# MLP residual seeded into PSUM, biases as bf16 products, layer norms on ScalarE, key products first, one table for Exp and Ln

## The reference

```python
# embedding: four tiers of rows, each with its own scale row, quantised to 16, 8, 6, 4 bits
scale = max(max(abs(tw[i] * ts[i])), 1e-8) / max_val        # over the whole tier
table = where(tier 0, tw * ts, clip(round(tw * ts / scale)) * scale)
x = layernorm(take(table, ids))
# mixer of a state space kind
proj = rms(x) @ in_proj_w.T                 # zgate 512, u 512, B 16, C 16, dt 8
xBC = silu(conv4(u, B, C))                  # 4 taps along the sequence
B, C = B * rsqrt(sum(B*B)), C * rsqrt(sum(C*C)); d = softplus(dt + dt_bias)
z = (z + d * (u*B - A*y)) / (1 + d*d*A); y = y + d * z;  out_t = y @ C     # 128 steps
x = x + ((out + D_skip*u) * silu(zgate)) @ out_proj_w.T + out_proj_b
# MLP, layer norm, quantised linear layer
x = x + gelu(rms(x) @ fc1_w.T + fc1_b) @ fc2_w.T + fc2_b
h = h + quantised_linear(layernorm(h))      # activation scale from the maximum over all rows
```

## Time and profile before

| | us |
|---|---|
| three runs | 1417.49, 1417.96, 1420.06 |
| median | 1417.96 |
| the profiled execution's own time | 1418.98 |
| its span, first to last instruction | 1417.2 |
| granted TensorE clock, mean | 0.954 |
| busy: TensorE, VectorE, ScalarE, GpSimd | 1148.7, 1181.0, 755.9, 802.1 |

### The profile page before, as it was taken

The page is one execution under the profiler, slowest core; times in us unless marked ns, Lnnn a source line. Parts: engine busy times, 40 slices in busy tenths (PEclk is TensorE's granted clock), DMA queues, the critical chain, the costliest instruction groups (busy, mean ns, idle before and its releaser), DMA issues. The chain is left out here.

```text
span 1417.2 us, 25541 instructions
## 1 busy us (share of the span) xinstructions
PE 1148.7 (81%) x7199; PEld 761.4 (54%) x7206; DVE 1181.0 (83%) x2167; ACT 755.9 (53%) x1108; POOL 802.1 (57%) x2246
## 2 busy tenths in 40 slices
PE   0595033499898989898989999898989898989766
PEld 0353021357575757475756566565657575757444
DVE  4899948788888988888888888889898988888277
ACT  4667343464646473737383738373646555551247
POOL 7870013485767667585858575857575858570100
PEclk9999996599999999999999999999999999999889
DMA  9999500000001010101010000000000000000015
GB/s 363 408 408 423 221 17 17 18 19 17 24 10 33 0 33 0 33 2 31 6 28 11 23 16 18 17 17 17 17 17 17 17 17 19 17 17 1 0 45 193
DMA packets 62069, 92.22 MB, mean 65 GB/s; under 512 B 9101, under 2 KB 55010, under 8 KB 57554
## 3 DMA queue, kind: packets, MB, share of 16 engines
q1 hardware_dynamic: 58386, 82.10, 16.3%
q0 software_dynamic: 3072, 8.39, 1.5%
q10 hardware_dynamic: 576, 1.31, 0.3%
HBM read 81.29 MB, written 10.49 MB: 65 GB/s over the span
## 5 line engine op out<-in xcount | busy, mean ns | idle before, releaser
L748 POOL TENSOR_TENSOR stp<-Gs,X 128x32 f32<-128x32 f32 x984 | 280.0, 285 | 270.1 <-ACT X L723 171.2
L750 POOL TENSOR_TENSOR Gs<-Gs,stp 128x32 f32<-128x32 f32 x984 | 279.5, 284 | 76.9
L605 PE MATMUL bank<-xT,w_in 128*128 128x512 f32 x512 | 242.3, 613 | 49.1 <-DVE uT L861 49.1
L1059 PE MATMUL bank<-mT,w_fc 128*128 128x512 f32 x512 | 244.0, 616 | 2.0 <-ACT mT L1047 2.0
L1078 PE MATMUL bank<-w_fc,gl 128*128 128x256 f32 x1024 | 243.1, 381 | 0.0
L1078 PEld LDWEIGHTS bank<-w_fc,gl 128*128 128x128 f32 x1024 | 191.0, 190 | 59.3 <-issue 32.0
L605 PEld LDWEIGHTS bank<-xT,w_in 128*128 128x128 f32 x512 | 93.8, 193 | 158.5 <-issue 87.8
L847 ACT ACTIVATE uT<-bank,cols 128x512 f32<-128x512 f32 x64 | 47.8, 775 | 211.3 <-DVE sz L973 163.5
L1059 PEld LDWEIGHTS bank<-mT,w_fc 128*128 128x128 f32 x512 | 99.5, 200 | 99.6 <-issue 94.8
L861 DVE SCALAR_TENSOR_TENSOR uT<-bank,cols,uT 128x500 f32<-128x500 f32 (+1 forms) x192 | 134.7, 738 | 2.3
L340 DVE TENSOR_TENSOR peak<-ring,peak 128x1536 f32<-128x1536 f32 (+2 forms) x67 | 115.3, 1722 | 19.8 <-ACT ring L243 18.4
(11 more groups left out here) (173 smaller groups left out, 1957.2 us busy)
## 6 DMA issues: line engine op xcount, KB each, us to landing
ring<-in_table SPq DMA_DIRECT2D x32, 1536.0 KB, 20.8
d_rep<-d_rows SPq DMA_DIRECT2D x128, 64.0 KB, 2.7
out<-res SPq DMA_DIRECT2D x16, 512.0 KB, 2.9
b_rep<-bc_rows SPq DMA_DIRECT2D x128, 32.0 KB, 1.8
c_rep<-bc_rows SPq DMA_DIRECT2D x128, 32.0 KB, 1.8
w_fc<-in_w_fc SPq DMA_DIRECT2D x2, 1024.0 KB, 8.7
w_in<-in_w_in ACTq DMA_DIRECT2D x1, 1088.0 KB, 5.1
h<-in_table,ids POOLq DMA_INDIRECT x64, 9.5
```

What stands on the lines that cost most here:

```text
L605: last = pe.matmul(dst, w_in[:, k, c0:c1], xT[:, k, :], start=(k == 0), stop=(k == KD - 1))
L748: pool.tensor_tensor(stp[:], Gs[:, t, ::-1, :], X2[:, t, :, :], ALU.mult).then_inc(rec.sem, 1)
L750: pool.tensor_tensor(Gs[:, t + 1, :, :], Gs[:, t, :, :], stp[:], ALU.add).then_inc(rec.sem, 1)
L1059: last = pe.matmul(pj[n % 4][:, :], w_fc1[:, k, n * P:(n + 1) * P], mT[:, k, :], start=(k == 0), stop=(k == KD - 1))
```

## The change

- **Residual of the MLP.** GpSimd's two additions are gone. ScalarE writes x2 into the two PSUM banks right after the transposed rows have been read from them (act_seed), and the second MLP product accumulates on top of it. For that the transposes are issued as products with their own start and stop flags.
- **Biases.** out_b and fc2_b are no longer 128-row tensors that are added, but bf16 rows: the value, its rest and the rest's rest stand in partitions 0, 64 and 96 of bias3 (made once, in turn 0, by dve_split_biases), and a product with pick, which has ones in those three rows, adds all three to a bank. It is one product per bank ahead of the output projection and one ahead of the second MLP product.
- **Norms on ScalarE.** The scaled rows for the projection (act_norm_rows), the layer norm that goes into the residual (act_layer_norm) and the centred rows for the maximum (act_x3, now one turn later, so that there is a `fourth` part and an eighteenth turn more) are activations with a bias and a scale per row. GpSimd makes the negative products that they need as biases.
- **Root of the MLP norm.** dve_rms's eleven instructions become two on GpSimd (pool_rms), after step 52 of the running recurrence (RMS_STEP), or after the last step where a turn has no `third` part.
- **Keys first.** dve_keys makes the two key products and the queries before it waits for the squares; GpSimd's next recurrence waits only for what reads Gs (kq 10, k_ready 2). bk is made at the start of the next turn.
- **Tables.** SiLU of the small channels comes before Exp, and Exp and Ln both use the set natural_log_exp_and_others. X is made after the third and fourth GELU, no longer after the fifth and sixth.
- **Order.** VectorE does the convolution of u right behind the gates, then x2, then the small normalisation, the maximum and the statistics.
- **Head.** Token scaling begins four tiles earlier (HOT_FROM 8 to 4), the small rest tile moves to the front, the last full tile is split in two, and the maxima of the two upper tiers are finished early (tier_top).

ScalarE in turn 15, from the small activations to the first GELUs, before. bc, dt and soft are the small channels, gl the GELU's output, utok the squares of the state.

The diff, cut to its core:

```diff
-            HOT_FROM = 8
+            HOT_FROM = 4
...
+                def tier_top(t0, t1):
+
+                    s = slice(t0, t1)
+                    dve.wait_ge(peak_step, folds[0])
+                    dve.tensor_tensor(peak[:, s, 0:3, :], peak[:, s, 0:3, :], peak[:, s, 3:6, :], ALU.max) \
+                        .then_inc(peak_step, 1)
+                    dve.wait_ge(peak_step, folds[0] + 1)
+                    dve.tensor_tensor(colmax[:, s, :], peak[:, s, 0, :], peak[:, s, 1, :], ALU.max) \
+                        .then_inc(peak_step, 1)
+                    dve.wait_ge(peak_step, folds[0] + 2)
+                    dve.tensor_tensor(colmax[:, s, :], colmax[:, s, :], peak[:, s, 2, :], ALU.max) \
+                        .then_inc(peak_step, 1)
+                    dve.wait_ge(peak_step, folds[0] + 3)
+                    dve.tensor_tensor(colmax[:, s, :], colmax[:, s, :], tsb[:, s, :], ALU.mult).then_inc(peak_step, 1)
+                    dve.wait_ge(peak_step, folds[0] + 4)
+                    folds[0] += 4
+                    dve.tensor_reduce(tmax[:, 1 + t0:1 + t1], colmax[:, s, :], AX.X, ALU.max,
+                                      apply_absolute_value=True).then_inc(tier_max, 1)
...
+        def dve_split_biases(dve):
+            whole = utok[:, 0:2, :]
+            rest = utok[:, 2:4, :]
+            dve.wait_ge(bias_in, 16)
+            dve.tensor_copy(bias3[:], whole).then_inc(halved, 1)
+            dve.wait_ge(halved, 1)
+            dve.tensor_tensor(rest[64:P], whole[64:P], bias3[64:P], ALU.subtract).then_inc(halved, 1)
+            dve.wait_ge(halved, 2)
+            dve.tensor_copy(bias3[64:P], rest[64:P]).then_inc(halved, 1)
+            dve.wait_ge(halved, 3)
+            dve.tensor_tensor(rest[96:P], rest[96:P], bias3[96:P], ALU.subtract).then_inc(halved, 1)
+            dve.wait_ge(halved, 4)
+            dve.tensor_copy(bias3[96:P], rest[96:P]).then_inc(halved, 1)
...
+        def act_norm_rows(act, g):
 
             if since(g):
-                dve.wait_ge(xr_T.sem, xr_T.at(g - 1))
+                act.wait_ge(xr_T.sem, xr_T.at(g - 1))
             if since(g, 3):
-                dve.wait_ge(xm_T.sem, xm_T.at(g - 3))
-            dve.wait_ge(ln.sem, ln.at(g))
+                act.wait_ge(xm_T.sem, xm_T.at(g - 3))
+            act.wait_ge(ln.sem, ln.at(g))
             for j in range(G):
-                dve.tensor_scalar(xr[:, j, :], rows(g, j), mv[:, j, 0:1], lnst[:, 6, j:j + 1],
-                                  ALU.subtract, ALU.mult).then_inc(xr_ready.sem, 1)
+                act.activation(xr[:, j, :], rows(g, j), ACT.Identity, bias=lnst[:, 7, j:j + 1],
+                               scale=lnst[:, 6, j:j + 1]).then_inc(xr_ready.sem, 1)
...
+            act.preload_act_table_set("natural_log_exp_and_others")
             act.wait_ge(dt_in.sem, dt_in.at(g))
             act.activation(soft[:], soft[:], ACT.Exp, scale=-1.0).then_inc(dt_act.sem, 1)
...
-                    pool.wait_ge(kq.sem, kq.at(g - 1))
-                    pool.wait_ge(k_ready.sem, k_ready.at(g - 1))
+                    pool.wait_ge(kq.sem, kq.at(g - 1, 10))
+                    pool.wait_ge(k_ready.sem, k_ready.at(g - 1, 2))
...
+        def act_layer_norm(act, g):
+            act.wait_ge(ln.sem, ln.at(g))
             if since(g):
-                dve.wait_ge(hx.sem, hx.at(g - 1, 1))
-                dve.wait_ge(xm_ready.sem, xm_ready.at(g - 1))
+                act.wait_ge(seeded.sem, seeded.at(g - 1))
+                act.wait_ge(xm_ready.sem, xm_ready.at(g - 1))
             for j in range(G):
-                dve.scalar_tensor_tensor(xl[:, j, :], rows(g, j), rs1[:, bass.ds(g * G + j, 1)], out_b[:],
-                                         ALU.mult, ALU.add).then_inc(xl_ready.sem, 1)
+                act.activation(xl[:, j, :], rows(g, j), ACT.Identity, bias=off1[:, bass.ds(g * G + j, 1)],
+                               scale=rs1[:, bass.ds(g * G + j, 1)]).then_inc(xl_ready.sem, 1)
...
+                pe.matmul(sbk[n][:, :], pick[:], bias3[:, OUT_B, :], start=True, stop=False, skip_group_check=True)
...
+        def pool_rms(pool, g):
+
+            pool.wait_ge(ssq_ready.sem, ssq_ready.at(g))
+            pool.tensor_tensor(ssq[:, 1, :], ssq[:, 0, :], eps6[:], ALU.add).then_inc(rsq.sem, 1)
+            pool.wait_ge(rsq.sem, rsq.at(g, 1))
+            pool.tensor_tensor(ssq[:, 2, :], ssq[:, 1, :], half[:], ALU.pow).then_inc(rsq.sem, 1)
...
+        def act_seed(act, g):
+
+            act.wait_ge(xmT_ready.sem, xmT_ready.at(g))
+            act.wait_ge(x2_ready.sem, x2_ready.at(g))
+            for n in range(2):
+                act.activation(sbk[n][:, :].rearrange("p (j c) -> p j c", j=2), xl[:, 2 * n:2 * n + 2, :], ACT.Copy) \
+                    .then_inc(seeded.sem, 1)
...
+                pe.wait_ge(seeded.sem, seeded.at(g))
+                for i in range(2):
+                    pe.matmul(sbk[i][:, :], pick[:], bias3[:, FC2_B, :], start=False, stop=False,
+                              skip_group_check=True)
...
-        def pool_residual(pool, g):
-            pool.wait_ge(x2_ready.sem, x2_ready.at(g))
-            pool.tensor_tensor(rows(g, 0, G), rows(g, 0, G), xl[:].rearrange("p j c -> p (j c)"), ALU.add) \
-                .then_inc(hx.sem, 1)
-
-            pool.drain()
-            pool.tensor_tensor(rows(g, 0, G).rearrange("p (j c) -> p j c", j=G),
-                               rows(g, 0, G).rearrange("p (j c) -> p j c", j=G),
-                               fc2_b[:].unsqueeze(1).to_broadcast([P, G, D]), ALU.add).then_inc(hx.sem, 1)
...
+        def act_x3(act, g, staged):
+
+            act.wait_ge(q_ready.sem, q_ready.at(staged))
+            if since(g):
+                act.wait_ge(mx.sem, mx.at(g - 1, 1))
+            act.wait_ge(ln3.sem, ln3.at(g))
             for j in range(G):
-                dve.tensor_scalar(tmp3[:, j, :], rows(g, j), mu3[:, bass.ds(g * G + j, 1)],
-                                  rs3[:, bass.ds(g * G + j, 1)], ALU.subtract, ALU.mult).then_inc(x3.sem, 1)
+                act.activation(tmp3[:, j, :], rows(g, j), ACT.Identity, bias=back3[:, j:j + 1],
+                               scale=rs3[:, bass.ds(g * G + j, 1)]).then_inc(x3.sem, 1)
...
+                    for hg in range(HG):
+                        dve_bk(dve, p, hg)
...
+                if first and third:
+                    pool_recurrence(pool, g, range(CL // 2, RMS_STEP))
+                    pool_rms(pool, p)
+                    pool_recurrence(pool, g, range(RMS_STEP, CL))
+                elif first:
+                    pool_recurrence(pool, g, range(CL // 2 if second else DVE_STEPS, CL))
+                if second and not (first and third):
+                    pool_rms(pool, p)
```

More of the change, by code:

```diff
@@ L1177, in turn @@
                         pe_fc2(pe, m, n - LEAD)
-                    if first and n == 6:
+                    if first and n == 2:
                         pe_ss(pe, g)
@@ L1195, in act_turn, with turn @@
         def act_turn(act):
-            def turn(g, first, second, third, nxt):
+            def turn(g, first, second, third, fourth, nxt):
                 p, m = g - 1, g - 2
@@ L1211, in turn @@
                     act_small_in(act, g)
+                if third:
+                    act_seed(act, m)
                 if first:
+                    act_small_silu(act, g)
                     act_small_dt(act, g)
+                if first and not third:
+                    act_small_norm(act, g)
+                    act_small_rsqrt(act, g)
                 for n in range(FT):
@@ L1275, in turn @@
                     dve_gate(dve, p, (2, 3))
+                if first:
+                    dve_conv_u(dve, g, (0, 1))
+                    dve_conv_u(dve, g, (2,))
+                if second:
+                    dve_x2(dve, p, 0)
+                if first:
+                    dve_conv_u(dve, g, (3,))
+                if second:
+                    dve_x2(dve, p, 1)
+                if first and second:
+                    dve_bc(dve, g)
+                if fourth:
+                    dve_max3(dve, g - 3)
                 if third:
@@ L1326, in _, with turn @@
             def _(sp):
-                def turn(g, first, second, third, nxt):
+                sp.dma_start(utok[:, 0:2, :], a["bias"].rearrange("p (i c) -> p i c", i=2)).then_inc(bias_in, 16)
+                def turn(g, first, second, third, fourth, nxt):
                     if first:
```

236 lines of the change are left out of this document (102 added, 134 removed).

## The result

The changed kernel takes 1383.28 us (median of 4 runs, 1378.12 to 1384.52), against 1417.76 (1417.49 to 1420.06) for the kernel before: ratio 0.9746, 95% interval 0.9719 to 0.9773, 34.5 us less. Forecast were 1401 and a range from 1384 to 1418: the sign is right, the gain is twice as large, and the time falls 0.7 us outside the range. The profiled execution took 1384.52 us with a span of 1382.7.

A forecast was written before the change was run, and what follows sets the result against it. Bound: a loop through GpSimd from T, each group's first recurrence step, to the next T. Turns -17.5, turn 1 +9.6, head -7.9, tail -4.0, 1.5 back, from 1418.98: 1400.7, predicted 1401 us, range 1384 to 1418.

The forecast's parts named there:

- Rival D: GpSimd reaches the root before the squares are there; slower than before from 1.6 us late, 1440 at 3 us; chance 0.09.
- The thirteen turns: Steady turns after turn 1: each falls from 68.26 to 66.9 us, -17.5 in all.
- the half recurrence: GpSimd's first half of the recurrence steps ends at T + 24.1: 21.1 of pitch and 3.0 lost to collisions with VectorE.
- The reordering: Key products ahead of the squares free the state at about T + 63, X is ready at T + 66.8: worth 0.
- Seeds in the leg: ScalarE's two copies of the residual into PSUM, between small activations and step size d: 1.1 us, ends 0.8 and 1.6.
- Turn 1: First full turn: root behind the whole recurrence, at T + 50.8, so 75.2 us against 65.6, +9.6.
- Head: Before the turns: folds end at 165.1 instead of 168.2 (-3.1), upper tiers -3.9, turn 0 -0.9; together -7.9 us.
- Tail: After the last T: root of group 15 5.0 us earlier, 1 perhaps from TensorE, +2.0 for hand-overs; -4.0 in all.
- TensorE's lag after turn 1: 1.5 us added back to the summed gain of -19.8 us, giving 1400.7.
- C: ScalarE's part shorter or X earlier, TensorE the bound at 64.6 to 65.6: 13 x -1.6, 1382 us; chance 0.13.
- B: GpSimd and VectorE collide where 0.3 us was given: 13 x 1.0 more, 1414 us; chance 0.17.
- E: No gain in the turn: an unseen handover keeps 68.2 us, the rest cancels to -1: 1418 us; chance 0.11.

The follow-up runs named there:

- number 1: The changed kernel with the root of the MLP norm after recurrence step 46 instead of 52: 1357.07 us.
- number 8: The kernel before with four extra matmuls of constants in TensorE's wait ahead of the MLP transposes: 1407.44 us, ratio 0.9919.
- number 7: The changed kernel with key and query products behind the sum of the squares again, GpSimd waiting for all of them: 1399.01 us.
- number 4: The changed kernel with the two copies of the residual into PSUM behind Exp and Ln instead of ahead of SiLU: 1377.68 us.
- numbers 13 and 14: The changed kernel with the root after step 46, in turn 1 too, with HOT_FROM 8 and with 4: 1344.91 and 1346.43 us.
- number 10: The changed kernel with the root after step 46, in turn 1 too, and both bias products left out: 1332.42 us.

## Why the forecast was half right

**Bound and loop: right.** The turn is set by the loop through GpSimd, as chosen, and not by TensorE (number 1) or VectorE. The root is reached without a wait:

```profile
640.24 0.25 POOL L789 TENSOR_TENSOR Gs<-Gs,stp 128x32 f32<-128x32 f32 x1
640.45 0.20 POOL L1047 TENSOR_TENSOR ssq<-ssq,eps 128x4 f32<-128x4 f32 x1
```

The squares were there at 636.2, T + 36.9, the forecast's 37. Rival D did not occur; number 1 could take 3.3 us of that room.

**The thirteen turns: -17.5 forecast, -37.3 measured.** This is the step that failed, by the size of its terms; the chain of legs itself was right. In the forecast's own terms, mean of the turns: T to the end of the root 42.5 for 43.2; root to small activations, "what they did", 4.8 for 5.4; to the end of d 4.9 for 5.0; to the next T 13.2 for 13.0; and the 0.3 added for the last steps and d's neighbours was not there. Together 1.5 us, times thirteen.

The 0.7 is the half recurrence: I took 24.1 for it from one turn, where the mean was 23.6 before and 23.0 after, that is 1.1 less; the norm factors up to the next step took 0.5 more than the 4.4. In the traces the 64 recurrence instructions of this half last 2.7 us a turn longer than their 0.25 each before and 2.1 after, where the forecast had 3.0. The excess beside VectorE's products of the gates (sz) fell from 1.2 to 0.7, and one of those products now stands beside the norm factors, of which one is:

```profile
624.36 0.52 POOL L595 TENSOR_TENSOR lnst<-lnst,eps 128x4 f32<-128x4 f32 x1
```

It took 0.20 before; here VectorE's product runs from 624.14 to 625.42. So where VectorE's work falls against GpSimd's is a part of the 0.7 that the forecast held fixed. The 0.6 is the small product: at the low clock it took 0.85 us longer in all thirteen old turns, and this clock came with TensorE's wait ahead of it, mostly 2.4 us before and 1.7 after, which number 8 filled and so brought 1.08 us into every turn. I had the row with the wait and the mean clock of 0.97, and took the product's duration for a constant.

**The reordering, "worth 0": true only for the forecast's own turn.** With the old order the last key product ends at T + 66.1 (number 7), ahead of the forecast T + 66.9 but behind the measured T + 65.4: 0.9 us a turn. The forecast had said that an earlier X would give it a worth; it did not ask how near that was.

**Seeds in the leg, 1.1: right as a term, too high as a price.** They fill 1.04 us of it (647.46 until SiLU at 648.50), but without them SiLU waits for VectorE, and only 0.2 is gained (number 4). The sum of 5.0 was right (4.90).

**Turn 1: right,** 74.2 against 75.2, with the root from T + 49.3 to T + 50.6 (50.8 forecast) and a low clock of 0.78.

**Head: -7.9 forecast, -2.5 measured.** The tops of the tiers gave their 3.9 (from the end of the folds to the scales 6.8 us instead of 10.7). VectorE's timeline, against the earlier trace rows, has the end of the folds and the token scales:

```profile
121.92 46.58 DVE L346 TENSOR_TENSOR peak<-ring,peak 128x1536 f32<-128x1536 f32 x26
168.53 0.96 DVE L352 TENSOR_TENSOR peak<-peak 128x768 f32<-128x768 f32 x1
...
174.21 1.15 DVE L412 SCALAR_TENSOR_TENSOR tok<-hot,small,tok 128x64 f32<-128x64 f32 x4
```

The folds ended at 168.5 and not 165.1, which the forecast had named as a sign of being wrong. One us is the last wait for gathered rows, which ended at 114.1 and not 113. The other 2.4 are a misreading of the earlier trace rows: its x16 are not eight tiles at 3.41 but seven and a half at 3.58 and a short rest of 81 rows,

```profile
167.75 0.42 DVE L340 TENSOR_TENSOR peak<-ring,peak 81x256 f32<-81x256 f32 x1
```

so fourteen tiles take 50.2 us and not 47.7; the 26 folds above are thirteen tiles at 3.58. VectorE's waits of 6.6 us for gathers were in the forecast as its start at 113; against HOT_FROM 8 they cost about a us (numbers 13 and 14). Turn 0 became 1.1 us longer rather than 0.9 shorter; this was not pursued.

**Tail: right in the sum,** -4.0. ScalarE's rows for group 15 start 94.9 us after the last T, 100.7 before:

```profile
1281.07 1.70 ACT L1058 ACTIVATE xr<-xl,ssq 128x256 f32<-128x256 f32 x4 [1.40 <-POOL ssq L1049]
```

The misses in the turns (-19.8), in the head (+5.4), in turn 1 (-1.0) and at the end (-0.8) sum to the -16 between forecast and profile. The end is the last stage's +0.7 less the 1.5 for TensorE's lag after turn 1, of which the marks show nothing. The forecast of 1401 also skipped its own last step: 1400.7 was for the profiled execution, and the median, 1.0 lower, would have been 1400.

**The rivals.** C's number is the measured one within 2 us, by luck: its first half, faster legs and an earlier X, happened, but its bound is refuted, since TensorE could still run the turn in 63.3 (and its 13 x -1.6 gives 1380, not 1382). B did occur on GpSimd's side (recurrence steps of up to 1.14 us under VectorE's bk), but behind the root and off the loop, since the next T comes 13 us later; d itself took 0.29. D and E did not occur.

## What to carry to other kernels

Follow the loop leg by leg and ask of each old duration what state it was measured in: a leg that stands behind an idle TensorE can hold its low clock, and a shorter wait can shorten the leg as well. Look, too, at what is ready just before the last releaser: in the old kernel the last key product was ready only 0.7 us before X let the next recurrence go, and it took over as soon as X came sooner (number 8). When a loop has been shortened, vary the one constant that places its work (here the step of the root): one line was worth 26 us, and it told loop from TensorE at once. And look at the first turn, where the steady order may not have been written down.

## What the runs showed of the hardware

A delay on the loop costs more than itself while TensorE waits for it: 1.27 us of a table load cost 1.53 a turn, rows 3.7 us later cost 4.7, because TensorE's clock was then 0.50 in more of the legs, or in more of each leg. The length of the wait alone does not decide it: 1.72 us was followed by 1.08 us for the small product in most turns and by 1.94 in the one at 969.8, 2.72 us by 1.08 in the one at 446.8; what else decides it is open. Extra matmuls in a wait can bring the high clock back (number 8). A bf16 bias product of 128x512 cost about 0.2 us (number 10, a quarter of 0.76), a ScalarE copy of 128x512 into PSUM 0.58.
